# Causal attention and top-2 expert routing on one core: VectorE's order around a tile's result, four memory sets on GpSimd, and the bank of the last attention values

## The chip, the cores and the metric

The kernel runs on one core of one Trainium2 chip. The metric is device microseconds (us) of one execution, lower is better.

## The reference

```python
xn = layernorm(x)                              # x: (2, 1024, 128) float32
k, q, v = (xn @ W.T + b for W, b in ...)       # 128 -> 128
a = softmax(causal(q @ k.T * 128 ** -0.5)) @ v
probs = softmax(xn @ Wr + br)                  # 16 experts
topv, topi = top_k(probs, 2)
h = relu(xn @ W1[e] + b1[e])                   # 128 -> 512
y = h @ W2[e] + b2[e]                          # 512 -> 128
out = x + a + sum over the two chosen e of topv * y
```

The reference computes every expert for every row. The kernel computes only the two that each row has chosen.

## The kernel before, in words

The input has 2048 rows, in 16 tiles of 128 (`NT`), 8 to each of the two sequences. The work has three stages.

**Attention and routing.** TensorE, VectorE and ScalarE normalise, project, score and weigh the 16 tiles. In the same time VectorE picks two experts a row and gives each of the 4096 (row, expert) pairs a place in a region of DRAM that belongs to its expert. GpSimd writes the rows there in 32 scatters (L470), each with a small memory set behind it that paces it. The regions are then read back in tiles of 128 rows that all have the same expert. There is room for `TILES` = 47 such tiles. How many hold rows depends on the routing, and the others are blank: the numbers of their rows lie outside the output, and their scatters write nothing.

**Experts.** For tile j TensorE runs `hidden(j)` (12 float16 matmuls, L1185 to L1187, with the first weights in a high and a low half), `result(j - 2)` (4 float32 matmuls of two passes each, L1198) and `slot_transpose(j + 3)` (L1153). It ends the round with `addresses(j + 1)`, work of its queue alone that reads expert numbers out of registers and computes weight addresses. ScalarE adds the bias and takes the relu (L609). VectorE has, in the order in which it is written: `slot_parts(j + 3)`, which splits a transposed tile into two float16 halves (L888, L889) and counts `xs_lo`; `y_of(j - 2)`, which scales the result out of PSUM into `ybuf` (L901) and counts `y_done`; and, for some j, `pairs_of` (L880, L881: where the rows of the next chunk of tiles belong), `low` (L807: the low half of an expert's first weights) and small steps for the gates. GpSimd waits for `y_done` and scatters `ybuf` to `pairs_dram` (L478). Behind each scatter stands a memory set of a scratch tile `tick` (L485), which counts `room_made`, and from the third tile on it first waits for the one before.

**Sums.** SyncE waits until the scatters of all tiles that hold rows have landed (L404; it has their numbers from the routing), reads `pairs_dram` back in eight loads (L406), and VectorE (L945, L949) and TensorE (L1236, added by L957) weigh the two results of each row with their gates and add them to `xin`. Eight stores (L410) write the output.

**Between attention and experts.** VectorE runs `low(2)`, `slot_parts(0)`, `slot_parts(1)`, `attended(15)` (L832: the last attention tile out of PSUM), `pairs_of(0)`, and then waits for some tables and reads the words that hold the tiles' expert numbers into registers (`words_on`, L319), which `y_of` needs. Only then does its loop begin, with `slot_parts(2)` and `slot_parts(3)`. TensorE runs the first four of the eight matmul pairs of attention tile 15 (`weigh(15, 0, FIRST)`), `slot_transpose(0)` and `(1)`, the other four, then `hidden(0)`, `slot_transpose(2)` and `(3)`, `hidden(1)`, and `slot_transpose(4)`. The last waits for the read of tiles 4 to 7 (`slots_in`, chunks are cut at `XG`) and for `xs_lo` of `slot_parts(2)`. All attention values go to one bank of PSUM, `pO[0]`, so `weigh(15, ...)` waits until VectorE has taken tile 14's out of it (`o_read`). The other bank, `pO[1]`, is used for counts and for the sums of squared weights, which VectorE has read when `scale_done` counts.

Of the kernel before, what the change touches and what calls it, by code (L numbers as in the profile page):

```python
# [15 lines left out]
P = 128  # L16
# [3 lines left out]
def attention_and_top2_experts(nc, x, Wk, bk, Wq, bq, Wv, bv, Wr, br, W1, b1, W2, b2, out):  # L20
    B, S, D = x.shape
# [3 lines left out]
    NT = B * S // P  # L25
    TB = S // P
    NCH = HID // P
    TILES = K * NT + E - 1
    EPS = 1e-5
    SCALE = float(D) ** -0.5  # L30
    G = 4
# [10 lines left out]
    NHB, NYB, NXS, NPB = 3, 6, 4, 4  # L42

    AHEAD = 3
    XG = [0, 2, 4, 8, 12, 24, 36, TILES]
    IDS = 12

# [28 lines left out]
    with ExitStack() as ctx:  # L76
# [6 lines left out]
        xin = sb("xin", [P, NT, D], F32)  # L83
# [233 lines left out]
        def words_on(engine):  # L317

            _, got = nc.values_load_multi_w_load_instructions(  # L319
                words[0:1, :], engines=[engine], min_val=0, max_val=16 ** IN_WORD - 1,  # L320
                skip_runtime_bounds_check_because="sums of numbers below 16")
            return got
# [93 lines left out]
        def _(pool):  # L416
# [57 lines left out]
            for j in range(TILES):  # L474
                if j in XG:
                    pool.wait_ge(pair_done, XG.index(j) + 1)
                pool.wait_ge(y_done, j + 1)
                pool.indirect_dma_start(pairs_dram, bass.IndirectOffsetOnAxis(ap=pair[:, j:j + 1], axis=0),  # L478
                                        ybuf[:, j % NYB, :], None, bounds_check=NT * P * K - 1,
                                        oob_is_err=False).then_inc(y_sent[j % NYB], 16)  # L480

                if j >= 2:
                    pool.wait_ge(room_made, j - 1)
                if j < TILES - 1:
                    pool.memset(tick[:, j % 2, :], 0.0).then_inc(room_made, 1)  # L485

        @block.scalar
# [135 lines left out]
        def _(dve):  # L623
# [205 lines left out]
            def attended(t):  # L829
                dve.wait_ge(rinv_done, t + 1)  # L830
                dve.wait_ge(o_done, t + 1)
                dve.scalar_tensor_tensor(out=xin[:, t, :], in0=pO[0][:, 0:D], scalar=rinv[:, t:t + 1],  # L832
                                         in1=xin[:, t, :], op0=ALU.mult, op1=ALU.add).then_inc(o_read, 1)

            row_max(0)
# [48 lines left out]
            def slot_parts(j):  # L884
                dve.wait_ge(xs_done, j + 1)
                if j >= NXS:
                    dve.wait_ge(l1_done, j - NXS + 1)
                step(dve.tensor_copy(xslot[:, j % NXS, 0, :], pT[j % 2][:, 0:D]))  # L888
                dve.tensor_tensor(xslot[:, j % NXS, 1, :], pT[j % 2][:, 0:D], xslot[:, j % NXS, 0, :],  # L889
                                  ALU.subtract).then_inc(xs_lo, 1)  # L890

            def y_of(j):
                e = dve.snap(expert_of(got, j), min_val=0, max_val=E - 1)
                factor = unscale[:, bass.ds(e, 1)]
                bias = b2t[:, bass.ds(e, 1), :].rearrange("p a d -> p (a d)")
                dve.lower_ap(factor)
                dve.lower_ap(bias)
                dve.wait_ge(l2_done, j + 1)
                if j >= NYB:
                    dve.wait_ge(y_sent[j % NYB], 16 * (j // NYB))  # L900
                dve.scalar_tensor_tensor(out=ybuf[:, j % NYB, :], in0=pO[j % 2][:, 0:D], scalar=factor, in1=bias,  # L901
                                         op0=ALU.mult, op1=ALU.add).then_inc(y_done, 1)

            def add_bias(g):
# [2 lines left out]
                dve.tensor_tensor(xin[:, here, :], xin[:, here, :], bvt[:, None, :].broadcast_to([P, G, D]),  # L907
                                  ALU.add).then_inc(biased, 1)

            slot_parts(0)  # L910
            slot_parts(1)
            attended(NT - 1)
            pairs_of(0)
            dve.wait_ge(erow_done, 1)
            dve.wait_ge(words_done, 1)
            dve.wait_ge(tables_done, 1)
            got = words_on(mybir.EngineType.DVE)
            dve.wait_ge(b2_in, 16)
            dve.wait_ge(bv_in, 16)
            dve.wait_ge(o_read, NT)  # L920
            for j in range(TILES):
                for i in range(j + AHEAD if j else 2, min(j + AHEAD + 1, TILES)):
                    slot_parts(i)
                if j >= 2:
                    y_of(j - 2)
                if j + 1 in XG[1:-1]:
                    pairs_of(XG.index(j + 1))
                for e in LOW_LATE.get(j, ()):
                    low(e)
                if j == GATES:  # L930
                    gaps()
                if j == GATES + 2:
                    gates()
                if j == GATES + 3:
                    sent_tiles()
                if j in ADDS:
                    add_bias(ADDS.index(j))
# [32 lines left out]
        def _(pe):  # L970
# [132 lines left out]
            def weigh(t, a, z):  # L1103

                i = t % TB
                for j in range(a, z):
                    ins = pe.matmul(pO[0][:, 0:D], probsT[t % 2][:, j // G, j % G * P:(j % G + 1) * P],  # L1107
                                    v[:, t // TB * TB + j, :], start=(j == 0), stop=(j == i))
                return ins

# [97 lines left out]

            pe.wait_ge(pt_act, NT)
            pe.wait_ge(pt_dve, sum(u % TB + 1 > G for u in range(NT)))  # L1210
            pe.wait_ge(o_read, NT - 1)
            weigh(NT - 1, 0, FIRST)
            slot_transpose(0)
            slot_transpose(1)
# [46 lines left out]
```

## Time and profile before

| What | us |
| --- | --- |
| Median of 3 runs | 169.4 |
| The 3 runs | 166.81, 169.40, 169.44 |
| The profiled execution, its own time | 166.94 |
| Its span, from the first instruction to the last | 165.2 |

The profile is of one execution. Around its span lie 1.74 us. PE is TensorE's matmuls, PEld its weight loads, DVE is VectorE, ACT ScalarE, POOL GpSimd, SP SyncE. A q behind an engine is its queue: waits, register work and issue. Times in rows are counted from the start of the span. The idle time in brackets is that of the engine just ahead of the instruction, with what ended it. Matmuls are pipelined, so the rows of PE overlap.

### The profile page before, as it was taken

Reading aid. Unit: us, or ns where it says so; the run is one execution under the profiler, and the core shown is the slowest. Engines: PE = TensorE matmul, PEld = TensorE weight load, DVE = VectorE, ACT = ScalarE, POOL = GpSimd, SP = SyncE. Lnnn points to the kernel's source line nnn. Section 1 sums busy time; section 2 is a strip of 40 time slices with the busy share of each in tenths; the row PEclk is TensorE's granted clock in tenths of the full one; section 3 lists DMA queues with packets and bytes.
Section 4 is the critical chain, followed back from the end, with each engine's and each line's share of the span. In section 5 each row is a group of like instructions: output and inputs, shape, how many; then the busy total and the mean of one; then the engine's idle time right before and its main releaser. Section 6 shows DMA issues by size and latency. Waiting matters only on the chain.

```text
span 165.2 us, 4999 instructions
## 1 busy us (share of the span) xinstructions
PE 148.2 (90%) x1384; PEld 131.5 (80%) x1384; DVE 114.5 (69%) x447; ACT 113.6 (69%) x335; POOL 118.0 (71%) x194
## 2 busy tenths in 40 slices
PE   5878989998599999669999999999999999999562
PEld 5645736677486778659999999999999999999462
DVE  1799767867867488378999978868555564552673
ACT  3486997998684667269898786887878767576000
POOL 7523878788788786000898888798989888888930
PEclk9999999999999999999999999999999999999985
DMA  4669999947113651365555441100010100001994
GB/s 142 164 214 408 404 409 412 352 95 277 55 36 97 174 118 48 68 126 106 121 121 129 116 114 59 40 1 29 32 54 16 37 30 30 30 30 42 290 334 131
DMA packets 24649, 22.69 MB, mean 137 GB/s; under 512 B 5649, under 2 KB 18331, under 8 KB 24496
## 3 DMA queue, kind: packets, MB, share of 16 engines
q1 hardware_dynamic: 22096, 18.14, 37.0%
q0 software_dynamic: 2528, 4.24, 7.4%
q8 instruction: 12, 0.20, 0.6%
q14 instruction: 13, 0.11, 0.2%
HBM read 16.02 MB, written 7.32 MB: 141 GB/s over the span
## 4 chain that ended last, share of the span: by engine, by line
POOL 42%; PE 22%; issue 17%; DMA 10%; DVE 5%; SPq 2%; DVEq 1%; ACT 1%; POOLq 0%
POOL slots_dram L470 18%; POOL pairs_dram L478 11%; PE pOO L1198 10%; POOL tick L472 6%; POOL tick L485 6%; DMA w<-pairs_dram 3%; PE pS L1185 2%; PE pS L1187 2%; PE pS L1186 2%; DMA xin<-in_L_attn_x 2%; DMA slots_dram<-rows,slotrow 2%; DMA slots<-slots_dram 1%; DMA pairs_dram<-ybuf,pair 1%; PE pT L1153 1%; SPq L406 1%
## 5 line engine op out<-in xcount | busy, mean ns | idle before, releaser
L609 ACT ACTIVATE xT<-pS,b1t 128x128 f32<-128x128 f32 x188 | 53.5, 373 | 20.9 <-PE pS L1187 18.8
L478 POOL DMA_INDIRECT pairs_dram<-ybuf,pair x47 | 46.4, 987 | 23.0 <-DVE ybuf L901 14.1
L1198 PE MATMUL pOO<-w,xT 128*128 x376 | 51.7, 281 | 0.0
L1198 PEld LDWEIGHTS pOO<-w,xT 128*128 128x128 f32 x376 | 45.5, 192 | 0.0
L470 POOL DMA_INDIRECT slots_dram<-rows,slotrow x32 | 31.3, 979 | 13.9 <-POOL tick L472 8.0
L1185 PE MATMUL pS<-xT,w1hi 128*128 128x128 f16 x188 | 33.9, 219 | 1.0 <-DVE w L807 0.8
L1187 PE MATMUL pS<-xT,w 128*128 128x128 f16 x188 | 33.9, 219 | 0.0
L1186 PE MATMUL pS<-xT,w1hi 128*128 128x128 f16 x188 | 33.9, 219 | 0.0
L888 DVE CAST xT<-pT 128x128 f16<-128x128 f32 x47 | 14.0, 298 | 19.1 <-PE pT L1153 18.7
L1107 PEld LDWEIGHTS pOO<-v,probsT 128*128 128x128 f32 x144 | 17.9, 191 | 9.1 <-issue 5.5
L485 POOL MEMSET tick<- 128x480 f32 x46 | 24.6, 534 | 0.0
L1107 PE MATMUL pOO<-v,probsT 128*128 128x128 f32 x144 | 19.5, 279 | 3.8 <-issue 2.2
L1185 PEld LDWEIGHTS pS<-xT,w1hi 128*128 x188 | 21.3, 113 | 1.5 <-DVE xT L889 1.0
L1186 PEld LDWEIGHTS pS<-xT,w1hi 128*128 x188 | 21.3, 113 | 0.0
L1187 PEld LDWEIGHTS pS<-xT,w 128*128 x188 | 21.3, 113 | 0.0
L901 DVE SCALAR_TENSOR_TENSOR ybuf<-pOO,unscale,b2t 128x128 f32<-128x128 f32 x47 | 16.5, 351 | 6.6 <-PE pOO L1198 4.3
L1074 PE MATMUL pS<-kT,qT 128*128 128x512 f32 (+3 forms) x48 | 18.0, 488 | 0.0
L567 ACT ACTIVATE probs<-pS,negm 128x128 f32<-128x128 f32 (+7 forms) x16 | 11.8, 740 | 7.8 <-DVE negm L813 7.2
L813 DVE CUSTOM_DVE_ANT_0 pS<-pS,causal 128x128 f32<-128x128 f32 (+7 forms) x16 | 12.2, 763 | 6.3 <-PE pS L1074 4.7
L889 DVE TENSOR_TENSOR xT<-pT,xT 128x128 f16<-128x128 f32 x47 | 13.7, 292 | 1.6
L1153 PE MATMUL pT<-ident,slots 128*128 128x128 f32 x47 | 12.6, 274 | 1.3 <-DMA slots<-slots_dram 0.7
L807 DVE SCALAR_TENSOR_TENSOR w<-w,wscale,w1hi 128x512 f16<-128x512 f32 x16 | 11.8, 745 | 0.0
(150 smaller groups left out, 221.4 us busy)
## 6 DMA issues: line engine op xcount, KB each, us to landing
w<-in_L_ffn_W SPq DMA_DIRECT2D x8, 1024.0 KB, 10.0
slots<-slots_dram SPq DMA_DIRECT2D x47, 65.0 KB, 2.0
w<-pairs_dram SPq DMA_DIRECT2D x8, 256.0 KB, 5.7
slots_dram<-slots SPq DMA_DIRECT2D x16, 65.0 KB
xin<-in_L_attn_x SPq DMA_DIRECT2D x4, 256.0 KB, 3.2
b2t<-in_L_ffn_b SPq DMA_DIRECT2D x1, 1024.0 KB
out<-xin SPq DMA_DIRECT2D x8, 128.0 KB, 2.4
pairs_dram<-ybuf,pair POOLq DMA_INDIRECT x47
```

Of the source, the lines that this page charges most:

```text
L470: pool.indirect_dma_start(slots_dram, bass.IndirectOffsetOnAxis(ap=slotrow[:, k, t:t + 1], axis=0), rows_i[:, t, :], None).then_inc(rows_s ...
L478: pool.indirect_dma_start(pairs_dram, bass.IndirectOffsetOnAxis(ap=pair[:, j:j + 1], axis=0), ybuf[:, j % NYB, :], None, bounds_check=NT * ...
L485: pool.memset(tick[:, j % 2, :], 0.0).then_inc(room_made, 1)
L609: ins = nc.scalar.activation(hid[:, j % NHB, here], pA(j)[:, here], ACT.Relu, bias=bias_of[c])
L901: dve.scalar_tensor_tensor(out=ybuf[:, j % NYB, :], in0=pO[j % 2][:, 0:D], scalar=factor, in1=bias, op0=ALU.mult, op1=ALU.add).then_inc(y_ ...
L1074: ins = pe.matmul(pS[t % 2][:, a:z], qT[:, t * P:(t + 1) * P], kT[:, at + a:at + z], start=True, stop=True)
L1107: ins = pe.matmul(pO[0][:, 0:D], probsT[t % 2][:, j // G, j % G * P:(j % G + 1) * P], v[:, t // TB * TB + j, :], start=(j == 0), stop=(j = ...
L1153: pe.transpose(pT[j % 2][:, 0:D], slots[:, j, 0:D], ident[:, :]).then_inc(xs_done, 1)
L1185: pe.matmul(to, w_hi, x_hi, start=True, stop=False)
L1186: pe.matmul(to, w_hi, x_lo, start=False, stop=False)
L1187: ins = pe.matmul(to, w_lo, x_hi, start=False, stop=True)
L1198: ins = pe.matmul(pO[r % 2][:, 0:D], hid[:, r % NHB, c * P:(c + 1) * P], second_weights(r, c), start=(c == 0), stop=(c == NCH - 1))
```

## The change

Four edits:

- On VectorE, each round of the expert loop runs `y_of(j - 2)` first and `slot_parts(j + 3)` second.
- VectorE reads its words of expert numbers ahead of `slot_parts(0)`, not behind `pairs_of(0)`.
- GpSimd has no memory set behind the scatters of tiles 42 to 46 (tile 46 had none), and doesn't wait for `room_made` there.
- The attention values of tile 15 go to `pO[1]`. TensorE waits for `scale_done` ahead of them, not for `o_read` of tile 14, and VectorE takes them from there.

```diff
+    CLOSE = 5
...
-                if j >= 2:
-                    pool.wait_ge(room_made, j - 1)
-                if j < TILES - 1:
+                if j < TILES - CLOSE:
+                    if j >= 2:
+                        pool.wait_ge(room_made, j - 1)
                     pool.memset(tick[:, j % 2, :], 0.0).then_inc(room_made, 1)
...
-                dve.scalar_tensor_tensor(out=xin[:, t, :], in0=pO[0][:, 0:D], scalar=rinv[:, t:t + 1],
+                dve.scalar_tensor_tensor(out=xin[:, t, :], in0=pO[t == NT - 1][:, 0:D], scalar=rinv[:, t:t + 1],
                                          in1=xin[:, t, :], op0=ALU.mult, op1=ALU.add).then_inc(o_read, 1)
...
+            dve.wait_ge(erow_done, 1)
+            dve.wait_ge(words_done, 1)
+            got = words_on(mybir.EngineType.DVE)
             slot_parts(0)
             slot_parts(1)
             attended(NT - 1)
             pairs_of(0)
-            dve.wait_ge(erow_done, 1)
-            dve.wait_ge(words_done, 1)
             dve.wait_ge(tables_done, 1)
-            got = words_on(mybir.EngineType.DVE)
             dve.wait_ge(b2_in, 16)
             dve.wait_ge(bv_in, 16)
             dve.wait_ge(o_read, NT)
             for j in range(TILES):
+                if j >= 2:
+                    y_of(j - 2)
                 for i in range(j + AHEAD if j else 2, min(j + AHEAD + 1, TILES)):
                     slot_parts(i)
-                if j >= 2:
-                    y_of(j - 2)
...
+                bank = pO[t == NT - 1]
                 for j in range(a, z):
-                    ins = pe.matmul(pO[0][:, 0:D], probsT[t % 2][:, j // G, j % G * P:(j % G + 1) * P],
+                    ins = pe.matmul(bank[:, 0:D], probsT[t % 2][:, j // G, j % G * P:(j % G + 1) * P],
                                     v[:, t // TB * TB + j, :], start=(j == 0), stop=(j == i))
...
-            pe.wait_ge(o_read, NT - 1)
+            pe.wait_ge(scale_done, 1)
             weigh(NT - 1, 0, FIRST)
```

What stands in a row on VectorE between attention and the loop, before. The names are tiles: `xT` holds the float16 halves, `pT` the transposed tile, `words` the expert numbers.

```order
L888 CAST xT<-pT 128x128 [waits xs_done]
L889 TENSOR_TENSOR xT<-pT,xT 128x128 [waits dve_step]
L832 SCALAR_TENSOR_TENSOR xin<-pOO,rinv,xin 128x128 [waits o_done,rinv_done]
L880 TENSOR_TENSOR second<-slots,erow 128x2 [waits slots_in0]
L881 TENSOR_TENSOR pair<-slots,second 128x2 [waits dve_step]
L319 TENSOR_LOAD words [waits tables_done,words_done,erow_done]
L888 CAST xT<-pT 128x128 [waits o_read,xs_done,bv_in,b2_in]
```

The same place in the changed kernel, whose lines are numbered one higher here:

```order
L320 TENSOR_LOAD words [waits words_done,erow_done]
L889 CAST xT<-pT 128x128 [waits xs_done]
L890 TENSOR_TENSOR xT<-pT,xT 128x128 [waits dve_step]
L889 CAST xT<-pT 128x128 [waits xs_done]
L890 TENSOR_TENSOR xT<-pT,xT 128x128 [waits dve_step]
L833 SCALAR_TENSOR_TENSOR xin<-pOO,rinv,xin 128x128 [waits o_done,rinv_done]
L881 TENSOR_TENSOR second<-slots,erow 128x2 [waits slots_in0]
L882 TENSOR_TENSOR pair<-slots,second 128x2 [waits dve_step]
L889 CAST xT<-pT 128x128 [waits o_read,bv_in,xs_done,b2_in,tables_done]
```

The read of the words has left the place between `pairs_of(0)` and the cast of `slot_parts(2)` and stands ahead of `slot_parts(0)`.

A round of VectorE's expert loop, before (the third, with `y_of(1)`; L896 and L897 compute the addresses of the scale and the bias):

```order
L888 CAST xT<-pT 128x128 [waits l1_done,xs_done]
L889 TENSOR_TENSOR xT<-pT,xT 128x128 [waits dve_step]
L896 ISA
L897 REGISTER_ALU
L901 SCALAR_TENSOR_TENSOR ybuf<-pOO,unscale,b2t 128x128 [waits l2_done]
```

And in the changed kernel:

```order
L897 ISA
L898 REGISTER_ALU
L902 SCALAR_TENSOR_TENSOR ybuf<-pOO,unscale,b2t 128x128 [waits l2_done]
L889 CAST xT<-pT 128x128 [waits l1_done,xs_done]
L890 TENSOR_TENSOR xT<-pT,xT 128x128 [waits dve_step]
```

The result of tile j - 2 is now taken ahead of the halves of tile j + 3.

## Rows read from the trace of the kernel before

**Rows 1.** The page: the chain that ended last, by engine.

```profile
POOL 42%; PE 22%; issue 17%; DMA 10%; DVE 5%; SPq 2%; DVEq 1%; ACT 1%; POOLq 0%
```

**Rows 2.** Busy time by stage: stretch, length, then each engine's (and instructions), clock, DMA.

```profile
69.60:75.30 5.70, 4.02 (x49) 3.53 (x50) 4.01 (x17) 3.39 (x10) 0.00 (x0) 1.00 0.52 111
75.30:151.60 76.30, 76.30 (x931) 76.22 (x929) 53.11 (x164) 60.29 (x205) 63.89 (x85) 1.00 0.23 61
```

**Rows 3.** The same for the result scatters of L478 alone, on POOL.

```profile
75.30:151.60 76.30, 42.28 (x43) 1.00 0.23 61
```

**Rows 4.** Timeline of VectorE, 66 to 76 us: start, length, instruction, idle time before.

```profile
70.04 0.29 DVE L888 CAST xT<-pT 128x128 f16<-128x128 f32 x1 [1.67 <-PE pT L1153]
...
71.56 0.16 DVE L881 TENSOR_TENSOR pair<-slots,second 128x2 int32<-128x2 int32 x1
72.73 0.29 DVE L888 CAST xT<-pT 128x128 f16<-128x128 f32 x1 [1.00 <-PE pT L1153]
73.06 0.29 DVE L889 TENSOR_TENSOR xT<-pT,xT 128x128 f16<-128x128 f32 x1
```

**Rows 5.** The chain in order of time: VectorE's queue reads the words.

```profile
71.67 0.84 DVEq L319
```

**Rows 6.** Timeline of TensorE, 66 to 77 us.

```profile
67.86 1.13 PE L1107 MATMUL pOO<-v,probsT 128*128 128x128 f32 x8 [0.60 <-DVE xin L832]
69.67 0.44 PE L1153 MATMUL pT<-ident,slots 128*128 128x128 f32 x2 [0.69 <-DMA slots<-slots_dram]
...
73.50 0.30 PE L1153 MATMUL pT<-ident,slots 128*128 128x128 f32 x1 [0.59 <-DVE xT L889]
74.64 0.22 PE L1185 MATMUL pS<-xT,w1hi 128*128 128x128 f16 x1 [0.84 <-DVE w L807]
```

**Rows 7.** L396 at 70.9 us alone, SyncE's read of tile 7: its landing.

```profile
L396 SPq DMA_DIRECT2D slots<-slots_dram x1: 333/333/333, 70.9 to 70.9; - x1
...
DMA to landing us min/median/max: 1.8/1.8/1.8
```

**Rows 8.** Timeline, 146 to 152 us: results of tiles 41 and 42.

```profile
146.10 1.11 PE L1198 MATMUL pOO<-w,xT 128*128 x8
...
147.83 1.11 PE L1198 MATMUL pOO<-w,xT 128*128 x8
...
147.96 0.35 DVE L901 SCALAR_TENSOR_TENSOR ybuf<-pOO,unscale,b2t 128x128 f32<-128x128 f32 x1
...
148.98 0.35 DVE L901 SCALAR_TENSOR_TENSOR ybuf<-pOO,unscale,b2t 128x128 f32<-128x128 f32 x1 [0.67 <-PE pOO L1198]
149.12 0.98 POOL L478 DMA_INDIRECT pairs_dram<-ybuf,pair  x1 [0.16 <-issue]
...
150.78 0.98 POOL L478 DMA_INDIRECT pairs_dram<-ybuf,pair  x1 [0.16 <-issue]
```

**Rows 9.** Timeline of VectorE and of GpSimd, 104 to 106 us: tile 15.

```profile
104.06 0.35 DVE L901 SCALAR_TENSOR_TENSOR ybuf<-pOO,unscale,b2t 128x128 f32<-128x128 f32 x1
...
105.19 0.98 POOL L478 DMA_INDIRECT pairs_dram<-ybuf,pair  x1 [1.04 <-DVE ybuf L901]
```

**Rows 10.** The chain in order of time, from 149 us on.

```profile
149.12 2.44 DMA pairs_dram<-ybuf,pair
...
153.91 5.53 DMA w<-pairs_dram
...
159.48 1.96 PE pS L1236 x8
```

**Rows 11.** Timeline of VectorE, 154 to 162 us: gates and results.

```profile
154.47 0.61 DVE L945 SCALAR_TENSOR_TENSOR xin<-w,gate,xin 128x128 f32<-128x128 f32 x2
...
160.07 0.61 DVE L945 SCALAR_TENSOR_TENSOR xin<-w,gate,xin 128x128 f32<-128x128 f32 x2 [0.21 <-DMA w<-pairs_dram]
```

**Rows 12.** The sums of L1236 alone: stretch, length, PE and PEld busy, clock, DMA.

```profile
157.20:158.50 1.30, 1.16 (x8) 0.97 (x8) 1.00 0.96 329
159.45:161.45 2.00, 1.97 (x10) 1.97 (x11) 0.55 1.07 311
```

## The prediction

> **What bounds the kernel now.** I read the page's chain first. GpSimd is on it for 42% of the span [rows 1], which sounds as if GpSimd set the time. Busy time by stage says otherwise for the expert stage: from 75.3 to 151.6 us TensorE is busy for all of 76.30 us at the full granted clock, VectorE for 53.11 and GpSimd for 63.89 [rows 2]. So the expert loop is TensorE's: from the result of tile 41 at 146.10 to that of tile 42 at 147.83 a round takes 1.73 us [rows 8]. GpSimd's own round, a scatter and a memory set back to back, is the 1.66 us from the scatter at 149.12 to that at 150.78 [rows 8]. It is 0.07 shorter, so GpSimd can only follow.
>
> What ends this stage is not TensorE's last result, though. Forty-three scatters start by 151.6 us [rows 3], so the one at 149.12 is that of tile 41. Its landing, 2.44 us later, is what SyncE waits for before it reads the results back [rows 10]: tiles 0 to 41 hold rows, and 42 to 46 are blank. The chain is therefore: hand-over from attention, 41 rounds of TensorE, y of tile 41 on VectorE, scatter 41, the loads, the sums, the stores. A microsecond counts if it comes off one of these links.
>
> Two links have slack in them that is only a matter of order. First the hand-over, 69.60 to 75.30, where TensorE is busy for 4.02 of 5.70 us [rows 2]. VectorE ends `pairs_of(0)` at 71.72 and starts the halves of tile 2 at 72.73 after 1.00 us of idle time [rows 4]. In it its queue reads the words for 0.84 us, 71.67 to 72.51 [rows 5]. The halves end at 73.35, and TensorE's transpose of tile 4, idle for 0.59, starts at 73.50 because of them [rows 4, 6]. Then TensorE's queue computes addresses, and `hidden(2)` starts 1.14 later, at 74.64 [rows 6]. From there on TensorE doesn't stop again. Second the result of tile 41: TensorE ends it at 146.10 + 1.11 = 147.21, and VectorE starts on it at 147.96, 0.75 late, because the halves of tile 46 come first. Tile 42 has no halves in front of it, and starts 148.98 - 148.94 = 0.04 behind its matmuls [rows 8].
>
> **The change, part by part.**
>
> Words early. Nothing is removed, 0.84 us of queue time is moved to a place where VectorE is idle: it waits 1.67 us for the slots before 70.04 [rows 4], and the read fits in. What is late next? The waits behind the read of the words took 72.73 - 72.51 = 0.22, and they stay. So the cast of tile 2 starts at about 71.72 + 0.22 = 71.94, and its halves end 0.62 later, at 72.56, which is 0.79 earlier. TensorE's transpose of tile 4 also waits for the read of tiles 4 to 7. Tile 7's was issued at 70.87 and landed 1.8 us later, at 72.69 [rows 7]. That is now the later of the two, and with the 0.14 that the transpose took to start behind its release, it starts at 72.82: 73.50 - 72.82 = 0.67 earlier. The queue's address work follows the transpose and moves with it, and `hidden(2)` with that. All rounds move by 0.67. The bounds are 0 (if tile 7's read lands at 73.35) and 0.79 (if it lands by 72.56). I take 0.67, the row's own landing.
>
> Result ahead of halves. y of tile 41 would end at 147.21 + 0.04 + 0.35 = 147.60 on the old clock, not at 148.31. The halves come later by 0.35 us less the wait that they had anyway, and they have time: `hidden(j + 3)` and the next transpose but one are more than a round of 1.73 away, and VectorE is idle for 0.67 in such a round [rows 8]. From y's end to the scatter GpSimd takes 105.19 - 104.42 = 0.77 where it was idle and waiting [rows 9]. For tile 41 that gave 148.31 + 0.77 = 149.08, and GpSimd's own round gave 149.12, so both bound it. Now, with the 0.67 of the first part, y ends at 146.93 and the scatter can start at 147.70: 1.42 earlier than 149.12, 0.67 of it from the words and 0.75 from the order.
>
> GpSimd must be able to follow. It last waited long at tile 15 (105.19), which VectorE's steps for the gates had delayed. From there 26 rounds of 1.66 make 148.35, which left 0.77 of slack to 149.12. Tile 15 moves too: y no longer stands behind a pair of halves, and its matmuls are 0.67 earlier. That is 0.67 + 0.6 at most in front of it, but the gate steps stay, so between 0.67 and 1.3. Scatter 41 could be reached by GpSimd at 148.35 - 0.67 = 147.68 at the latest, beside 147.70 by y. It is close, and I let y decide. If scatter 15 didn't move at all, scatter 41 would start at 148.35 and the gain be 0.77.
>
> No memory set behind the last scatters. Tiles 42 to 46 are blank, and nothing in the chain waits for them: SyncE's wait is for 41. It could only act through what it shares with VectorE. L945, which reads two SBUF operands, takes 0.61 for two at 154.47, beside GpSimd, and 0.61 for two at 160.07, when GpSimd is done: from tile 42 at 150.78, four more rounds of 1.66 put its last scatter at 157.42 [rows 8, 11]. So the cover isn't needed, and I take 0. The range is 0 to 0.1. The Trainium skill speaks for more: its page "GPSIMD Engine Reference", section "8. Key points", says that GpSimd shares its SBUF interfaces with VectorE and contends with VectorE's instructions that have two SBUF inputs. By that rule a pair beside a memory set would be longer than one without, which these rows don't show, and the removed sets would give something on top of the sum.
>
> Other bank. `weigh(15, 0, FIRST)` waited 0.60 for VectorE to empty the bank and started at 67.86. It can now start about 0.55 earlier, but the transpose behind it waits for the slots until 69.67 anyway [rows 6]. The gain is hidden: 0. It makes TensorE's idle time before 69.67 one piece of about 1.2 us, in place of 0.60 and 0.69.
>
> The tail. The loads are issued and land 1.42 earlier. Does anything hold? VectorE's first gates start behind y of tile 46, which is TensorE's and moves only by 0.67, so 154.47 becomes 153.80. They end 0.75 later against the loads, and the waits for loads behind them, such as the 0.21 at 160.07 [rows 11], must take that up. They are there because the last loads land about 5.5 us after their issue, up to 159.44 and beyond [rows 10]. TensorE's sums that started at 159.48 did so on the loads too [rows 10]. They ran at about half the clock, 1.96 us in place of 1.16 for eight [rows 10, 12]. If the clock falls no earlier than now less 0.67, these eight are done in front of VectorE's four instructions from 160.07 on, twice 0.61 and two short gaps, which ended at about 161.33. The sums ended at 161.44, so at most 0.11 is won. I take 0.1.
>
> Sum: 0.67 + 0.75 + 0 + 0 + 0.1 = 1.5 us. The profiled execution took 166.94, so 165.4 us. It lies near the lowest of the three runs, 166.81. The other two, 169.40 and 169.44, are 2.5 higher, and by the same sum they give 167.9. I forecast the profile's level and let the range reach to the other. By 1.5 of 166.9 the change is worth 0.9%, and about 2% is what a measurement of this kernel can tell from no change.
>
> **The rivals.**
>
> The slots' read decides the hand-over. If tile 7 lands at about 73.3, the words' move gives nothing and only 0.75 + 0.1 is left: 166.1. For it: the landing is only 0.67 before the old release, and landings of this line differ by some tenths. Against it: SyncE issues those reads by itself, and nothing of the change touches it.
>
> GpSimd's own round decides the end. Price: scatter 41 at 148.35, a gain of 0.77 + 0.1, or 166.1. For it: its slack is 0.77 now, and the memory sets behind tiles 15 to 41 stay. Against it: y of tile 15 moves with TensorE.
>
> Slower: the clock falls in the hand-over. TensorE's matmuls before 69.67 now end earlier and leave one gap of 1.2 us. If the granted clock drops to its lower level, 1.2 GHz, and the loop starts at it, matmuls take some 1.7 times as long (1.96 against 1.16 [rows 10, 12]). About 5 us at that level cost 2.6 us, as much as lies between the runs of 166.8 and 169.4, and 2.6 - 1.5 = 1.1 makes 168.0. The point from which it decides is 3 us at the lower level. Against it: the clock was 1.00 through the same stage with 1.29 us of idle time in two pieces [rows 2, 6], and the gaps at 73.50 get shorter. "TensorE: Matmul & The Clock Gate" in the Trainium skill, section "What's actually happening", says that the throttled state is the default and that the moment of a change differs from run to run. By that rule a gap that did no harm in this profile can do some in another run.
>
> The change doesn't do what it says: VectorE's y comes no earlier, because its queue's address work (L896) now stands bare in front of it. That would take back some 0.3 us: 165.7. In a loop with 0.67 of idle time a round the queue has the time to do it ahead.
>
> **How the numbers follow.** Forecast 165.4 us, 0.6. Slots' read 0.1, GpSimd's round 0.1, clock 0.1, bare address work 0.1. Low end: the read of the slots lands early (0.12 more), the sets' 0.1 and the spread of fast runs, about 0.5: 164.5. High end: the two rivals at 166.1 and the clock's 168.0, which is also the upper runs' level less the gain: 168.0. Faster by over 2% would need 163.6 at the profile's level, or the upper level before against the lower after: 0.08. Slower by over 2% needs more than 170: 0.03. Within 2%: 0.89.
>
> **What would show it.** VectorE's cast for tile 2 at 71.9 with no idle time of 1.00 in front, the transpose of tile 4 at about 72.8 released by the DMA, `hidden(2)` at about 74.0. y of tile 41 starting 0.04 behind its matmuls. Scatter 41 at 147.7 and the first load at 150.2. TensorE still busy for all of the loop at clock 1.00. The forecast is wrong if the round of TensorE grows over 1.73 us because halves come late, if scatter 41 starts 1.66 behind scatter 40 with y long done, or if the stores end no earlier although the loads do.

## The result and the profile after

| | before | after |
| --- | --- | --- |
| Median, us | 167.21 (11 runs) | 165.35 (11 runs) |
| Lowest to highest, us | 166.56 to 169.44 | 164.56 to 166.34 |
| The profiled execution, us | 166.94 | 164.81 |
| Its span, us | 165.2 | 163.1 |

The changed kernel takes 0.9888 of the time before, with a 95% interval of 0.9857 to 0.992. The forecast was 165.4 us. The ratio leaves out the two slow runs of before near 169.4, and the median in the table has them in.

The page's chain by engine, after. It answers to [rows 1]:

```profile
PE 56%; POOL 25%; issue 7%; DVE 5%; DMA 3%; ACT 0%; SPq 0%; POOLq 0%
```

TensorE now holds 56% of the chain and GpSimd 25%. Busy time by stage, columns as in [rows 2], and stretches moved with the loop:

```profile
66.00:69.60 3.60, 2.12 (x19) 1.93 (x18) 1.50 (x5) 1.04 (x2) 0.00 (x0) 1.00 0.30 60
69.60:75.30 5.70, 4.52 (x55) 4.15 (x56) 4.66 (x17) 3.43 (x11) 0.00 (x0) 1.00 0.53 113
74.00:150.20 76.20, 76.20 (x932) 76.20 (x933) 49.85 (x167) 61.36 (x207) 65.00 (x85) 1.00 0.23 61
```

TensorE is busy for 4.52 of 5.70 us in the hand-over, where it was 4.02, and still for all of the loop, at a granted clock of 1.00 throughout. VectorE's timeline there, the answer to [rows 4]:

```profile
70.20 0.29 DVE L889 CAST xT<-pT 128x128 f16<-128x128 f32 x1 [1.85 <-PE pT L1155]
...
71.72 0.16 DVE L882 TENSOR_TENSOR pair<-slots,second 128x2 int32<-128x2 int32 x1
72.09 0.29 DVE L889 CAST xT<-pT 128x128 f16<-128x128 f32 x1 [0.20 <-PE pT L1155]
72.41 0.29 DVE L890 TENSOR_TENSOR xT<-pT,xT 128x128 f16<-128x128 f32 x1
```

The idle time of 1.00 us ahead of the cast of tile 2 is 0.20. TensorE's timeline, the answer to [rows 6]:

```profile
69.83 0.44 PE L1155 MATMUL pT<-ident,slots 128*128 128x128 f32 x2 [1.71 <-DMA slots<-slots_dram]
...
72.90 0.28 PE L1155 MATMUL pT<-ident,slots 128*128 128x128 f32 x1
73.96 0.22 PE L1187 MATMUL pS<-xT,w1hi 128*128 128x128 f16 x1 [0.78 <-DVE w L808]
```

The transpose of tile 4 no longer waits (it has no bracket), and `hidden(2)` starts at 73.96 where it was 74.64. The bracket there names `low(3)` (L808), but it isn't what `hidden(2)` waited for: that needs three low halves, and the third was done ahead of `slot_parts(0)`. TensorE's queue computed addresses from 72.87 to 73.79 and went on without a pause. `hidden(1)` had started at 72.23, so `hidden(2)` follows it by one round of 1.73 us, where before it was 2.57 (72.07 to 74.64). The timeline around the result of tile 41, the answer to [rows 8]:

```profile
145.39 1.11 PE L1200 MATMUL pOO<-w,xT 128*128 x8
...
146.54 0.35 DVE L902 SCALAR_TENSOR_TENSOR ybuf<-pOO,unscale,b2t 128x128 f32<-128x128 f32 x1 [0.85 <-PE pOO L1200]
146.81 0.28 DVE L889 CAST xT<-pT 128x128 f16<-128x128 f32 x1
...
147.67 0.98 POOL L479 DMA_INDIRECT pairs_dram<-ybuf,pair  x1 [0.23 <-issue]
```

The matmuls end at 145.39 + 1.11 = 146.50 and VectorE starts 0.04 later, with the cast behind it. Scatter 41 starts at 147.67 and the first load is issued at 149.90. Up to here every mark is within 0.3 us of the forecast's.

The end is another matter. The forecast followed the chain of the page, which ends with VectorE's sums and the stores behind them. But two queues end the kernel before together. These are the last scatter (timeline of GpSimd) of before:

```profile
157.42 0.98 POOL L478 DMA_INDIRECT pairs_dram<-ybuf,pair  x1 [0.17 <-issue]
```

and the drains. A `DRAIN` stands at the end of the program in the queue of each engine; behind it there are only a few semaphore instructions. (The view lists all instructions of that line: duration in ns, then its start in us.)

```profile
L76 POOLq DRAIN  x1: 9186/9186/9186, 155.8 to 155.8; - x1
...
L76 SPq DRAIN  x1: 7/7/7, 165.0 to 165.0; - x1
```

GpSimd's ended at 155.8 + 9.2 = 165.0, SyncE's, behind the stores, at 165.0. Of after, the last three scatters and the same drains:

```profile
152.62 0.98 POOL L479 DMA_INDIRECT pairs_dram<-ybuf,pair  x1 [0.63 <-issue]
153.91 1.11 POOL L479 DMA_INDIRECT pairs_dram<-ybuf,pair  x1 [0.30 <-DVE ybuf L902]
155.32 0.98 POOL L479 DMA_INDIRECT pairs_dram<-ybuf,pair  x1 [0.30 <-issue]
```

```profile
L77 POOLq DRAIN  x1: 8652/8652/8652, 154.2 to 154.2; - x1
...
L77 SPq DRAIN  x1: 7/7/7, 162.4 to 162.4; - x1
```

SyncE is done at 162.4 and GpSimd at 154.2 + 8.65 = 162.8, which is 6.5 us behind the end of a scatter that writes nothing. The last semaphore instructions of all engines stand at 163.0. So this execution of the changed kernel ends 6.5 us behind the scatter of a blank tile.

### The profile page after: what moved, and what is told of

Its sections match the earlier page's. It is cut to its first block, busy times and chain, and to the rows that moved or that the text cites. A ratio compares the mean times of both kernels' runs of the same rounds, so it can differ in the third digit from the quotient of the medians.

```text
span 163.1 us, 4994 instructions
## 1 busy us (share of the span) xinstructions
PE 147.1 (90%) x1384; PEld 130.8 (80%) x1384; DVE 110.3 (68%) x447; ACT 113.7 (70%) x335; POOL 117.2 (72%) x190
## 4 chain that ended last, share of the span: by engine, by line
PE 56%; POOL 25%; issue 7%; DVE 5%; DMA 3%; ACT 0%; SPq 0%; POOLq 0%
PE pOO L1200 27%; POOL slots_dram L471 18%; PE pS L1187 7%; PE pS L1189 6%; PE pS L1188 6%; POOL tick L473 6%; PE pT L1155 3%; PE pS L976 3%; DVE xin L950 2%; DMA slots_dram<-rows,slotrow 2%; DVE xin L946 2%; DMA slots<-slots_dram 1%; PE pS L1027 1%; DVE xin L958 1%; PE pOO L999 1%
## 5 line engine op out<-in xcount | busy, mean ns | idle before, releaser
L479 POOL DMA_INDIRECT pairs_dram<-ybuf,pair x47 | 47.7, 1015 | 21.7 <-DVE ybuf L902 12.0
L486 POOL MEMSET tick<- 128x480 f32 x42 | 22.4, 533 | 0.0
L889 DVE CAST xT<-pT 128x128 f16<-128x128 f32 x47 | 13.2, 280 | 2.1 <-PE pT L1155 2.1
L560 ACT ACTIVATE w1hi<-w,wscale 128x512 f16<-128x512 f32 x16 | 11.9, 756 | 0.0
```

## The experiments

Theories: (A) each part is worth what the forecast says (words 0.67, result first 0.75, sets 0, bank 0); (B) the hand-over's gain is lost to the slots' read; (C) the removed sets act too; (D) the drain, formed on the profile above ahead of all experiments: the program ends when the later of two sides does, the stores or GpSimd's drain, and the drain ends 6.5 us behind GpSimd's last scatter. Ratios are to the kernel before, from runs on the same chip, and 1% is 1.67 us.

**Each part alone.** The words:

```diff
+            dve.wait_ge(erow_done, 1)
+            dve.wait_ge(words_done, 1)
+            got = words_on(mybir.EngineType.DVE)
             slot_parts(0)
...
-            dve.wait_ge(erow_done, 1)
-            dve.wait_ge(words_done, 1)
             dve.wait_ge(tables_done, 1)
-            got = words_on(mybir.EngineType.DVE)
```

> Kernel before with the words read early, alone. Forecast's theory: the halves of tile 2 end at about 72.6, tile 4's transpose starts at about 72.8 released by the read of the slots, hidden(2) at about 74.0, and everything behind moves by 0.67: span 164.5, ratio 0.996. Rival (the read of the slots decides the hand-over): transpose stays near 73.3 and the span moves by under 0.2.

Measured: 166.27 us, ratio 0.9929 (0.9895 to 0.9963). TensorE's timeline of this kernel:

```profile
74.04 0.22 PE L1185 MATMUL pS<-xT,w1hi 128*128 128x128 f16 x1 [0.78 <-DVE w L807]
```

`hidden(2)` starts 0.60 earlier than before, scatter 41 at 148.50 (0.62 earlier). By the ratio it gave 1.2 us, with 0.6 to 1.75 as the interval, which holds the 0.67. The span is 164.6, as expected (164.5), and here too GpSimd's drain ended it: 164.3, against 163.7 for SyncE.

The result ahead of the halves:

```diff
+                if j >= 2:
+                    y_of(j - 2)
                 for i in range(j + AHEAD if j else 2, min(j + AHEAD + 1, TILES)):
                     slot_parts(i)
-                if j >= 2:
-                    y_of(j - 2)
```

> Kernel before with the result ahead of the halves, alone. Forecast's theory: TensorE's rounds unchanged at 1.73 us, y of tile 41 starts 0.04 behind its matmuls, its scatter at 148.4 and the first load at 150.8 or a little before, span 0.75 shorter, 164.5, ratio 0.9955. Rival (halves come late): TensorE's round grows over 1.73. Rival (GpSimd's own round decides): scatter 41 at 149.1 in spite of y.

Measured: 166.64 us, ratio 0.9979 (0.9942 to 1.0016): a gain of 0.35 us, between -0.3 and 1.0. The two medians, 167.12 and 166.64, are 0.48 apart. The timeline of VectorE, GpSimd and SyncE's queue:

```profile
147.32 0.35 DVE L901 SCALAR_TENSOR_TENSOR ybuf<-pOO,unscale,b2t 128x128 f32<-128x128 f32 x1 [0.85 <-PE pOO L1198]
...
148.45 0.98 POOL L478 DMA_INDIRECT pairs_dram<-ybuf,pair  x1 [0.23 <-issue]
...
151.55 3.67 SPq L406 DMA_DIRECT2D w<-pairs_dram  x8
```

VectorE does what the forecast says: 147.32 in place of 147.96. Scatter 41 follows, 0.67 earlier. But the first load is issued 3.10 us behind the scatter's start, where before it was 2.51 (151.63 - 149.12), so it comes only 0.08 earlier. The last scatter ends 0.51 earlier, at 157.89. SyncE ends last, at 165.1, and the span of this execution is 165.3, no shorter than before.

No sets behind the last scatters:

```diff
-                if j >= 2:
-                    pool.wait_ge(room_made, j - 1)
-                if j < TILES - 1:
+                if j < TILES - 5:
+                    if j >= 2:
+                        pool.wait_ge(room_made, j - 1)
                     pool.memset(tick[:, j % 2, :], 0.0).then_inc(room_made, 1)
```

> Kernel before without the memory sets behind the last five scatters, alone. Forecast's theory: 0, ratio 1.000, as nothing waits for blank tiles. Second theory, formed on the trace of the changed kernel: GpSimd's drain ends some 6.55 us behind its last scatter and is the last event of the span. In before SyncE's last store and that drain end together at 164.97, so the drain should now end at about 163.4 and SyncE's path alone hold the end: span 165.0 to 165.2, ratio 1.000 too. The two differ in the time of the drain only.

Measured: 166.35 us, ratio 0.9944 (0.9903 to 0.9985). The interval lies below 1: the sets were worth 0.9 us (0.25 to 1.6), where the forecast had 0. The expectation with D had a ratio of 1.000 as well, so neither foresaw the time. What D foresaw is the drain's. Nothing before scatter 41 moved (149.19). What moved are the last scatter, here in GpSimd's timeline, and the drain behind it, in the line of the program's end:

```profile
156.10 1.02 POOL L478 DMA_INDIRECT pairs_dram<-ybuf,pair  x1 [0.30 <-issue]
```

```profile
L76 POOLq DRAIN  x1: 8753/8753/8753, 155.0 to 155.0; - x1
...
L76 SPq DRAIN  x1: 7/7/7, 164.1 to 164.1; - x1
```

The last scatter ends at 157.1 in place of 158.4 and the drain at 163.7 in place of 165.0. Now the stores end last, at 164.1. They too are 0.8 earlier, because the last load landed at 159.90 and not at 160.71. Over the traces of all kernels that landing varies by more, so this run doesn't tell whether it belongs to the sets. The earlier end of GpSimd's side does: four sets less, and from scatter 41 to scatter 46 it is 6.91 us in place of 8.30.

The other bank (the three lines of the diff that name `pO` or `scale_done`):

> Kernel before with the other bank for the last attention values, alone. All theories: TensorE's first four pairs of attention tile 15 start about 0.5 earlier, the transpose behind them still waits for the slots until about 69.7, time unchanged, ratio 1.000. The clock rival: the idle piece of 1.2 to 1.7 us lowers the granted clock in the rounds behind it in some execution, which would be 1 us or more longer.

Measured: 167.31 us, ratio 1.001 (0.9968 to 1.0052). Nothing, as forecast. This run also tests the rival of the clock. In TensorE's timeline the gaps become one:

```profile
66.80 2.06 PE L1107 MATMUL pOO<-v,probsT 128*128 128x128 f32 x17
70.82 0.44 PE L1153 MATMUL pT<-ident,slots 128*128 128x128 f32 x2 [1.96 <-DMA slots<-slots_dram]
```

It is 1.96 us long, since the reads of the slots went out late in this execution (tile 7's at 71.97, before at 70.87). The stretch that follows, by its busy times and clock:

```profile
68.00:78.00 10.00, 6.44 (x75) 5.75 (x74) 6.01 (x20) 4.74 (x15) 0.00 (x0) 1.00 0.46 101
```

The granted clock stays at 1.00, its upper level of 2.4 GHz.

**Each part taken out of the changed kernel.** The same diffs, undone. The words:

> Changed kernel with the words read late again. Forecast's theory: the whole hand-over falls back by 0.67, span 163.1 + 0.7 = 163.8 and ratio to before about 0.992. Drain theory: the last scatter is behind y of tile 46, which is TensorE's, so the drain moves by the same 0.7: 163.8 as well.

Measured: 166.10 us, 0.9932 (0.9899 to 0.9965), 0.44% above the changed kernel's 0.9888: 0.73 us for the words, though the two intervals still overlap a little. The span is 163.9 (163.8 expected), and `hidden(2)` is 2.58 us behind `hidden(1)` again.

The result and the halves:

> Changed kernel with the halves ahead of the result again. Forecast's theory: scatter 41 at about 148.4, first load at 150.8, VectorE waits for loads again in the sums, span 163.1 + 0.75 = 163.9 or up to 164.5 if the loads are as slow as in before. Drain theory: the drain stays at about 162.8, and SyncE's last store, not the drain, ends the span.

Measured: 165.78 us, 0.9897 (0.9857 to 0.9936). In the changed kernel the order of result and halves is worth 0.1% by the ratios and 0.43 us by the medians (165.78, 165.35), which isn't told from nothing. As D said, SyncE ends last, at 164.1. But the drain isn't at 162.8, it is at 163.8: in this execution y of tile 44 started only at 152.56, though y of tile 43 started at the same time as in the kernel with the shorter tail below (150.28, 150.29), where tile 44's is at 151.91. The last scatters are late with it. No row shows why.

The sets:

> Changed kernel with all memory sets. Forecast's theory (nothing waits for blank tiles): span as the changed kernel's, 163.1, ratio 0.989. Drain theory: scatters 42 to 46 go at 1.66 from 149.4, the last ends at about 157.0, the drain at 163.6, span 163.8, ratio 0.993, with VectorE's last instruction still ending near 160.3.

Measured: 165.86 us, 0.9914 (0.988 to 0.9948), 0.26% above: 0.4 us, in intervals that overlap. Here is the end of its profiled execution, the slowest of the eight (166.68):

```profile
157.19 0.98 POOL L478 DMA_INDIRECT pairs_dram<-ybuf,pair  x1 [0.17 <-issue]
```

```profile
L76 POOLq DRAIN  x1: 9188/9188/9188, 155.5 to 155.5; - x1
...
L76 SPq DRAIN  x1: 7/7/7, 163.5 to 163.5; - x1
```

VectorE ended its sums at 161.4 and SyncE at 163.5, and yet the span went on to 164.9: GpSimd's drain ended at 164.7. In this execution the stores' gain was lost to it. Not all of its lateness is the sets': scatter 41 had started 1.10 us later than in the changed kernel (148.77), in part for a long round of TensorE that is told of below, and from there to the last scatter it took 8.42 us in place of 7.65. So the sets account for 0.77.

**The drain, put to the test.** First from the side of the stores: TensorE also sums the one group of results that VectorE had to itself, so that VectorE's tail is shorter and the drain is not touched.

```diff
-            return TYL * c + (c == NPE - 1), TYL * c + TYL
+            return TYL * c, TYL * c + TYL
...
-            combine(NPE - 1, range(TYL * (NPE - 1), summed(NPE - 1)[0])).then_inc(shared_done, 1)
-            dve.wait_ge(shared_done, 1)
```

> Changed kernel with the sum of row tile 6 moved from VectorE (two instructions of 0.35 us) to TensorE, which has its idle time there. If VectorE's chain of sums, which no longer waits in the changed kernel, ends the span, it is 0.5 us shorter (VectorE ends at 159.8 and so does the span, 162.6). Drain theory: VectorE ends 0.5 earlier, the span stays at 163.1, as the drain ends at 162.8 whatever VectorE does.

Measured: 165.36 us, 0.9897 (0.9863 to 0.9931). From the start of y of tile 46 to the end of VectorE's work it took 160.21 - 153.69 = 6.52 us, 0.5 less than the 7.01 of the changed kernel (160.29 - 153.28), and the time is the same (165.36 for 165.35). The drain ended at 163.25, 0.6 behind SyncE's 162.63.

Second, the last scatter alone made late, in the changed kernel. It is a blank tile's, so nobody waits for it:

```diff
+                if j == TILES - 1:
+                    pool.wait_ge(room_made, TILES - 5)
+                    for _ in range(3):
+                        step(pool.memset(tick[:, 0, :], 0.0))
                 pool.indirect_dma_start(pairs_dram
```

> Changed kernel with three memory sets, one after the other, in front of the last scatter, that of blank tile 46. No other engine waits for it before the end. Forecast's theory: nothing, span 163.1 to 164. Drain theory: the last scatter starts 1.6 to 2.0 us later, GpSimd's drain ends 6.53 behind its end, and the span grows by the same 1.6 to 2.0, to about 165 (ratio to before about 1.000), with VectorE's last instruction still near 160.3.

Measured: 166.75 us, 0.9983 (0.9948 to 1.0018). The gain of the change is gone but for 0.2%. GpSimd's timeline and the drains:

```profile
154.84 1.65 POOL L481 MEMSET tick<- 128x480 f32 x3
157.26 0.98 POOL L482 DMA_INDIRECT pairs_dram<-ybuf,pair  x1 [0.77 <-POOL tick L481]
```

```profile
L76 POOLq DRAIN  x1: 7740/7740/7740, 157.0 to 157.0; - x1
...
L76 SPq DRAIN  x1: 7/7/7, 163.5 to 163.5; - x1
```

The last scatter starts 157.26 - 155.32 = 1.94 later than in the changed kernel, and the span is 1.94 longer (165.01 against 163.07). Scatter 41 starts at 147.51, no later than there, and VectorE ends at 161.4. SyncE's own side is 1.1 later in this execution (163.5 for 162.4), but GpSimd's, at 164.8, is later still. Nine of the ten executions lie between 166.59 and 166.94, and the lowest is 2.03 above the lowest of the changed kernel. This is the run that shows D.

Third, no scatters of blank tiles. This kernel has the shorter tail too, and leaves out the scatters of tiles 42 to 46, which write nothing for this input, and SyncE's waits for them:

```diff
-                sp.wait_ge(y_sent[n], 16 * len(range(n, TILES, NYB)))
+                sp.wait_ge(y_sent[n], 16 * len(range(n, TILES - 5, NYB)))
...
-            for j in range(TILES):
+            for j in range(TILES - 5):
```

> Changed kernel with the sum of row tile 6 on TensorE and without the scatters of tiles 42 to 46, which hold no rows for this input (for another routing they would). Drain theory: the drain ends near 155 and SyncE's last store ends the span, about 0.6 to 0.9 shorter than with those scatters, 162.4 to 162.8, ratio to before 0.985. Forecast's theory: their scatters cost nothing, ratio as with them, 0.990.

Measured: 165.10 us, 0.9866 (0.9833 to 0.9899). The drains:

```profile
L76 POOLq DRAIN  x1: 7832/7832/7832, 147.3 to 147.3; - x1
...
L76 SPq DRAIN  x1: 7/7/7, 163.3 to 163.3; - x1
```

GpSimd's drain is over at 155.1, 8 us ahead of the end, and the stores set it at 163.3. So the drain holds nothing up any more, and the time falls by 0.3% against the kernel with the shorter tail alone (0.9866 against 0.9897), with intervals that overlap. The expectation was 0.6 to 0.9 us, and the profiled span isn't shorter (163.6 against 163.5). The side of the stores lies close to the drain's: here the first load went out 2.84 us behind scatter 41 and the last landed 9.0 behind that.

**GpSimd's round.** The rival "GpSimd's own round decides" rests on a margin of 0.07 us. The scratch tile is made 640 words wide, not 480:

```diff
-        tick = sb("tick", [P, 2, 480], F32)
+        tick = sb("tick", [P, 2, 640], F32)
```

> Changed kernel with memory sets of 640 columns instead of 480, 0.67 us each instead of 0.53. GpSimd's round is then 1.80 us, above TensorE's 1.73. If that margin of 0.07 is what keeps GpSimd off the chain, scatters fall behind y from the start, scatter 41 starts at about 77.0 + 41 * 1.80 = 150.8 in place of 147.7, VectorE waits for loads again, and the span is 2 to 3 us longer, 165 to 166. If GpSimd has other slack, nothing changes.

Measured: 169.50 us, 1.0142 (1.0087 to 1.0197). GpSimd's timeline:

```profile
149.90 0.98 POOL L478 DMA_INDIRECT pairs_dram<-ybuf,pair  x1 [0.16 <-issue]
150.87 0.67 POOL L485 MEMSET tick<- 128x640 f32 x1
151.69 0.98 POOL L478 DMA_INDIRECT pairs_dram<-ybuf,pair  x1 [0.17 <-issue]
```

The set takes 0.67 in place of 0.53 and the round 1.79, more than TensorE's 1.73. Scatter 41 starts at 151.69, 4.0 later than in the changed kernel, though y of tile 41 starts at 146.92. The span is 4.2 longer, where 2 to 3 were expected. So the margin is real and under 0.14 us.

**The small steps.** In the trace of the changed kernel with the sets put back, one round of TensorE took 2.35 us. In three other traces one or two rounds at the same place took 1.83 to 1.98. Shortly before, VectorE has four steps of six elements, of which three are shown. GpSimd's timeline there, then VectorE's:

```profile
102.04 0.98 POOL L478 DMA_INDIRECT pairs_dram<-ybuf,pair  x1 [0.27 <-issue]
103.01 0.53 POOL L485 MEMSET tick<- 128x480 f32 x1
...
102.45 0.57 DVE L739 TENSOR_SCALAR sent_of<-sent_of 128x6 f32<-128x6 f32 x1
...
103.06 0.51 DVE L741 TENSOR_SCALAR sent_of<-sent_of 128x6 f32<-128x6 f32 x1
103.61 0.17 DVE L742 TENSOR_SCALAR erow<-sent_of 128x6 int32<-128x6 f32 x1
```

Alone such a step takes 0.17 us. The one at 102.45 ends at 103.02, with the scatter, and the one at 103.06 ends at 103.57, just behind the set. That the long steps are what stretched the round isn't shown. The next kernel spreads the four steps over four rounds of the changed one (each step is followed by a `yield`, which the cut below leaves out):

```diff
                 if j == GATES + 3:
-                    sent_tiles()
+                    sent_steps = sent_tiles()
+                if j in (GATES + 3, GATES + 6, GATES + 8, GATES + 10):
+                    next(sent_steps)
```

> Changed kernel with the four small steps that compute how many scatters to wait for put one each into rounds 16, 19, 21 and 23 in place of all four in round 16. In some traces one or two of them took 0.51 to 0.74 us for six elements beside GpSimd, not 0.17, which made y of tile 15 late and in one trace stopped TensorE for 0.6 us in round 19. If that is a cost of the changed kernel, TensorE's rounds are all 1.73 or less and the median falls by 0.1 to 0.3 us; otherwise it is the same, 0.989.

Measured: 165.34 us, 0.9896 (0.9866 to 0.9927), the same. The steps took 0.26, 0.35, 0.35 and 0.16, and no round there was stretched. But none was in the trace of the changed kernel either, where one step took 0.67. VectorE has 0.85 us of idle time a round (the bracket of the row at 146.54), room for such a step.

At its end this kernel is the changed one, and its profiled execution ended with the stores: SyncE's drain at 163.35, GpSimd's at 163.0. Its first load went out 2.74 us behind scatter 41, where the changed kernel's took 2.23. So which side of the changed kernel ends last differs from execution to execution.

None of these kernels is clearly faster than the changed one.

## Why the forecast held, and where it didn't

**The bound.** TensorE's rounds set the loop: right. It stays busy for all of it, at 1.00.

**Words early, 0.67.** Right in place and size. The cast starts at 72.09 (71.94 forecast), the transpose at 72.90 (72.82), `hidden(2)` at 73.96 (74.0). Taken out, it costs 0.73 us; put in alone, it gives 0.6 to 1.75. But the step that sized it was not what happened. Tile 7's read landed at 72.31, earlier than the 72.69 taken over, and the halves of tile 2 ended at 72.70, so neither held the transpose. It stood directly behind the matmuls of `hidden(1)`: TensorE had no wait left there. Counted from `hidden(1)` the gain is 0.84 (1.73 for 2.57), and 0.16 of it went because `hidden(1)` itself started later in this execution (72.23 for 72.07). That the two ways give the same 73.96 is luck.

**Result ahead of halves, 0.75.** The mechanism was right, the worth was not. y starts 0.04 behind its matmuls, and scatter 41 comes 0.67 earlier by this part alone. By the two ratios only 0.35 and 0.15 us arrive at the end, by the medians 0.48 and 0.43. The intervals don't exclude 0.75, so it is the traces that say why it should be less. The step that failed is "A microsecond counts if it comes off one of these links", which took the chain of the loads as the only one. The time from scatter 41's start to the first load differs between 2.23 and 3.10 us over the traces, whatever the kernel, which hid the gain in this part's own trace. And GpSimd's drain can cap it. In the changed kernel the last scatter stands behind y of tile 46, which has no halves ahead of it and doesn't move with the order (154.07 in this part's own trace, 154.00 before). One reading of the forecast was of the wrong round: the 0.67 us of idle time stand in a round without halves. Rounds with halves have 0.66 to 0.78 us ahead of the cast, so nothing changes by it.

**No sets, 0.** Wrong, and the same step. The forecast said that nothing in the chain waits for the blank tiles. The end of the program does, through GpSimd's drain. In the kernel before both ends lay at 165.0. The part is worth 0.25 to 1.6 us by itself, and about 0.4 in the changed kernel, where the two intervals overlap. The rows that would have told were in the trace of before: the last scatter at 157.42 and the drain behind it, which the page's chain doesn't show because it follows one end only. Beside VectorE the sets did nothing that was seen: the pairs of L946 take 0.60 to 0.61 us both beside scatters and after them, and those of the kernel before, beside scatters and sets, 0.61 to 0.62. The Trainium skill's page "GPSIMD Engine Reference", section "8. Key points", which the forecast weighed, says that the two engines contend when VectorE's instruction has two inputs in SBUF, as these have. VectorE's rows don't show it. GpSimd's do: the scatter at 153.91 began inside the first of these pairs and took 1.11 us in place of 0.98:

```profile
153.55 0.61 DVE L946 SCALAR_TENSOR_TENSOR xin<-w,gate,xin 128x128 f32<-128x128 f32 x2
```

It is the scatters that pay. The sets take 0.50 to 0.55 us beside such instructions and up to 0.55 without them, so this isn't where the gain comes from.

**Bank, 0, and the tail, 0.1.** The bank: right. In the tail the forecast expected VectorE's waits for loads to take up 0.75. They were gone altogether, all 0.38 + 0.55 + 0.21 = 1.14 us of them: it runs from 153.55 to 160.29 without a bracket, 2.57 us earlier than before at its end. TensorE's sums, which the forecast had at half the clock, ended at 158.64, and the granted clock from 157 to 160 us was 1.00. Of the 2.57, 0.4 went to the drain, since the span became only 2.13 shorter. This profiled execution is a lucky one: its loads landed earlier than those of most other traces, and at 164.81 it is 0.54 below the median.

**The sum.** 1.5 was forecast, 1.86 is the difference of the medians, 1.87 is what the ratio gives, and 0.9888 of the profiled 166.94 is 165.1. Two errors lie in it, one of each sign: the order of the result probably put too high, by about 0.4 going by its ratio alone, and the sets too low by 0.4 to 0.9. That the time was met within 0.1 us is in part luck, and it hides that the gain was put 0.4 too low: the forecast started from the profiled 166.94, and the median of before is 167.21.

**The rivals.** The slots' read: not so, see above. GpSimd's round: not in the changed kernel, since scatter 41 started where y let it (147.67, forecast 147.70), but 0.14 us more a round made it so. The clock: idle pieces of 1.71 and 1.96 us ahead of the hand-over, both longer than the 1.2 feared, left it at 1.00 in the two profiled executions. Its price was worked out wrong: where matmuls take 1.7 times as long, 5 us at the lower level cost 5 - 5 / 1.7 = 2.1 us and not 2.6, and it decides from 3.6 us on and not from 3. Bare address work: no, y starts 0.04 behind TensorE.

What stays open: what GpSimd's drain does for 6.5 us; how often it and how often the stores end the changed kernel; why a scatter's landing differs by 0.9 us and the last load's by 1.2 (8.0 to 9.2 us behind the first issue, and 9.0 in the kernel without blank scatters, so these aren't the cause); and whether the parts' small effects add up, since the product of the four alone is 0.986 and the whole 0.9888.

## What to carry to other kernels

Each of these executions ended when the last of the queues was done, not when the output was written. Ask of each engine when its last instruction ends and what the drain behind it costs, above all where an engine issues transfers that nobody needs: two ends at the same place hide each other, and then the gain of an edit on one of them is capped by the other. And when a forecast comes out right, test its terms one by one, since errors of both signs can cancel.

## What the runs showed of the hardware

- **GpSimd's drain.** In all 14 traces it ended 6.53 to 6.82 us behind the end of its last indirect scatter, however late that was (148.45 to 159.63), and also where the scatter writes nothing. The span ended about 0.2 us behind the later of GpSimd's and SyncE's drains. GpSimd's was the later in six of the traces (by up to 1.3 us), SyncE's in seven, and in that of the kernel before they ended together.
- **Small operations beside GpSimd.** A six-element TENSOR_SCALAR took 0.16 to 0.17 us alone and up to 0.74 beside GpSimd (kernel before, GpSimd's timeline and VectorE's):

```profile
102.65 0.98 POOL L478 DMA_INDIRECT pairs_dram<-ybuf,pair  x1 [0.30 <-issue]
...
102.89 0.74 DVE L742 TENSOR_SCALAR erow<-sent_of 128x6 int32<-128x6 f32 x1
```

  The Trainium skill's page "SBUF — State Buffer", section "Who interferes with whom", says that this operation can take the pair of ports that VectorE shares with GpSimd, and that whoever comes second is fully blocked. By that rule a step of 0.17 waits for an instruction of GpSimd, whatever its own size. The traces agree for most steps: each of those that took 0.26 us or more ended within 0.04 us of the end of a scatter or a set, as here at 103.63. They don't agree for all of a scatter's time: a step that started at most 0.16 us behind the start of a scatter took 0.17 to 0.22 (in the changed kernel one at 101.41, with the scatter at 101.31).
- **Scatters beside VectorE.** Over the 14 traces 79 result scatters began inside a VectorE instruction of 128 columns or more with two inputs in SBUF that had 0.15 us or more to go. 74 of them took 1.02 to 1.31 us. Of the other 574 none took more than 1.00.
- **A scatter's pace.** Without a set between, one starts 1.29 and 1.41 us behind the other (152.62, 153.91, 155.32). With the 0.53 us set between them it is 1.66, though scatter and set together were busy for 1.51. Where both scatters take 0.98, the set costs 1.66 - 1.29 = 0.37, not 0.53.
